# Masked score banks written by ScalarE, queries spread over heads by four transfers a group, and y normalised by GpSimd, in a fused attention and mixture-of-experts layer

## The chip, the cores and the metric

The kernel is one program on one core of a Trainium2 chip. Its time is the device time of one execution in microseconds (us). Three executions of the kernel before took 561.37, 568.28 and 562.6 us, a median of 562.6 us.

## The reference

The input is 4 sequences of 1024 tokens with 256 features, float32. One layer is computed:

```python
x = x + attention(layernorm(x), Wq, Wk, Wv, Wo)   # 16 heads of 16, window of 64 keys, causal
x = x + ffn(layernorm(x), ...)                    # 8 experts, 2 chosen per token, plus a shared expert
# attention: scores = q.k / sqrt(16) + bias; bias is 0 where i-64 < j <= i, else -inf; softmax over j; times v; times Wo
```

Norms have eps 1e-5 and no gain. The router takes the sigmoid of its logits, and an expert's output is scaled by the mean of its tokens' weights. Only the attention part is touched by the change; the experts' part follows it and is the same in both kernels.

## The kernel before

**Tiling.** The attention runs as a sweep over 16 groups `g` of 256 tokens (`step` on every engine, called by `sweep`). A group has 4 blocks `n` of 64 queries; `b = 4g + n` numbers the blocks, 64 in all. A block of 64 queries needs 128 keys, its own 64 and the 64 before. Since the queries of four heads are laid as a block diagonal against the keys (`bd`), a block's scores for 16 heads are one tile of 128 keys x 1024 (head, query) columns. It fills two PSUM banks; there are two such pairs, `S[0]` and `S[1]`, used in turn. In a sequence's first block the first 64 keys are masked out altogether (`mask_first`), in all others the window mask applies (`window_mask`).

**A block on TensorE** (`step`, L726). The scores of block b+1 come first (`scores_of`, L617): two bf16 matmuls write the mask into the banks, for the keys' upper and lower 64 rows (L621), and the products add to it (L626). They wait for `s_P`, the exponentials of block b-1, which had the same banks. Then `shift_of` (L642) subtracts the row maxima from block b. It waits for two transfers that SyncE (SP) issues, of the negated maxima's high and low parts (L331). Then come the products of the probabilities of block b-1 with v (`pv_of`, L656), the first half of a projection for the next group (q at n=0, k at n=1, v at n=2; L567), the transpose of block b+1's maxima (`maxima_T`, L637), the transposes of the products with v (`pvT_of`, L665), the second half of the projection, the output projection (`wo_of`, at n=1 and 2), and the transpose of the block's output (`oT_of`, L671). At n=0 the four transposes of the normalised tokens for the experts stand between `pvT_of` and the second half (`zT_of`, L578); at n=3 those of the tokens for the group after next stand there (`yT_of`, L578), and in the place of a projection the routing logits (L703, L710).

**VectorE** reads the scores for their maxima (L1221, `rmax`), reduces the transposed maxima (L1226, `negm`, and L1229, `neglo`), divides by the softmax sum, forms the low parts of values that are multiplied in two float32r parts (L1194, L1245), and does statistics, residuals and routing. **ScalarE** does the exponentials (L1015), the copies out of PSUM (`pvs` L1022, the high parts L977 and L1027, q, k and v), the copy of the routing logits (L1039, `parts`), at n=3 of groups 2 to 11 a weight cast (L1074, `wF`), the normalisation of y for the group after next (L1033, at n=0), and the spread of q into `bd`: four multiplications of the whole `qs` by a column of ones and zeros per head (L1000; one at n=0, three at n=1). **GpSimd** computes 1/std (L448, L450) and the product that L1033 adds as its bias (L447, L454), the places of routed rows, and issues the indirect transfers that scatter them (L511). SP issues, besides the maxima, at n=1 a load of expert weights (L326) and the store of the transposed tokens (L338).

**Order.** Each engine's instructions stand in the order in which the functions call them; semaphores join the engines. Nothing else reorders them.

## Time and profile before

| | |
|---|---|
| executions (us) | 561.37, 568.28, 562.6; median 562.6 |
| profiled execution (us) | 568.08, span 566.3 |
| granted TensorE clock, mean | 0.976 of full speed |
| busy: PE, VectorE, ScalarE, GpSimd | 93%, 69%, 60%, 40% of the span |
| the sweep over the 16 groups | from about 17 to 334 us of the span |

The span runs from the first to the last instruction of the profiled execution; the rest of its time lies around it. PE is TensorE's matmul, PEld its weight load, DVE VectorE, ACT ScalarE, POOL GpSimd, and SPq the transfers that SyncE issues. An engine's busy time is the sum of its instructions, and says nothing on what it waits for.

### The profile page before, as it was taken

The page shows a single profiled execution, that of the slowest core. Times are in us where ns is not written, and L with a number is a line of the kernel's source. Part 1 is how long each engine was busy: PE and PEld are TensorE (multiplying, and loading weights), DVE is VectorE, ACT ScalarE, POOL GpSimd, SP SyncE. Part 2 cuts the span into 40 slices and gives each one's busy share as a digit, 9 for nine tenths or more (in the row PEclk, how much of TensorE's full clock was granted, in tenths as well). Part 3 has the DMA queues.
Part 4 walks back from the last instruction along what each step waited for, and adds up shares of the span by engine and source line. Part 5 has one row for each costly group of instructions (what it writes and reads, how often), then busy time and mean ns, then how long its engine had stood idle before and what let it go on. Part 6 is the DMA issues. An engine that isn't in the chain of part 4 may idle for free.

```text
span 566.3 us, 16447 instructions
## 1 busy us (share of the span) xinstructions
PE 526.6 (93%) x5561; PEld 422.5 (75%) x5561; DVE 390.3 (69%) x1207; ACT 337.2 (60%) x776; POOL 227.5 (40%) x419
## 2 busy tenths in 40 slices
PE   7899999899999899999989868889999999989997
PEld 4567877676776687677777546878888887769996
DVE  6566688788788788778767646666666665542764
ACT  4667787776777687677676423316676666551111
POOL 5100112244245335424423426723555555443661
PEclk9899999989999999999998977999999999998999
DMA  6260101311321320321121114777555454425994
...
DMA packets 42559, 69.16 MB, mean 122 GB/s; under 512 B 9708, under 2 KB 28655, under 8 KB 42480
## 3 DMA queue, kind: packets, MB, share of 16 engines
...
q14 instruction: 31, 0.25, 0.1%
...
## 4 chain that ended last, share of the span: by engine, by line
PE 80%; ACT 7%; DVE 5%; issue 4%; another core or an unknown queue 2%; DMA 0%; POOL 0%; SPq 0%; ACTq 0%; DVEq 0%; POOLq 0%
PE ps L567 40%; PE ps L626 8%; PE ps L656 6%; PE ps L820 5%; PE ps L911 3%; PE ps L665 3%; PE ps L621 3%; PE ps L578 2%; PE ps L642 2%; ACT probs L1015 2%; PE ps L671 2%; PE ps L710 2%; PE ps L928 1%; ACT vm L988 1%
## 5 line engine op out<-in xcount | busy, mean ns | idle before, releaser
L511 POOL DMA_INDIRECT z_slots<-z,slot x64 | 64.5, 1008 | 120.6 <-PE ps L626 100.3
L567 PE MATMUL ps<-wF,wA 128*128 x639 | 105.6, 304 | 1.7 <-DVE wA L1551 1.0
L552 POOL DMA_INDIRECT y_rows<-vm,dest x71 | 69.6, 980 | 72.5 <-issue 37.8
L567 PEld LDWEIGHTS ps<-wF,wA 128*128 128x128 f32 x639 | 85.2, 189 | 14.3 <-issue 6.2
L1221 DVE TRANSPOSE_TENSOR_REDUCE rmax<-ps 128x32 f32<-128x1024 f32 x64 | 79.6, 1244 | 17.9 <-PE ps L626 16.6
L1015 ACT ACTIVATE probs<-ps 128x1024 f32<-128x1024 f32 x64 | 65.6, 1025 | 34.8 <-PE ps L642 33.9
L626 PE MATMUL ps<-bd,kT 64*128 64x256 f32 x512 | 68.9, 391 | 0.0
L567 PE MATMUL ps<-yT,wA 128*128 128x256 f32 x384 | 61.9, 299 | 1.5 <-DVE yT L1194 1.5
L626 PEld LDWEIGHTS ps<-bd,kT 64*128 64x128 f32 x512 | 51.5, 198 | 5.7
L567 PEld LDWEIGHTS ps<-yT,wA 128*128 128x128 f32 x384 | 50.0, 191 | 4.6 <-issue 1.9
L1119 ACT ACTIVATE vt<-ps 128x256 f32<-128x256 f32 x32 | 12.3, 383 | 56.1 <-PE ps L567 56.1
L1226 DVE TENSOR_REDUCE negm<-ps 32x32 f32<-32x128 f32 x64 | 17.8, 278 | 39.0 <-PE ps L637 29.4
L1551 DVE TENSOR_TENSOR wA<-ps,wA 128x256 fp32r<-128x256 f32 x71 | 30.1, 424 | 20.7 <-issue 11.9
L1000 ACT ACTIVATE bd<-qs,cst 128x512 f32<-128x512 f32 x62 | 43.2, 723 | 0.1
L1160 ACT ACTIVATE vt<-ps 128x128 f32<-128x128 f32 x71 | 19.8, 279 | 38.8 <-PE ps L567 32.4
L1557 DVE TENSOR_TENSOR vt<-vt,ps 128x128 f32<-128x128 f32 x71 | 20.3, 286 | 28.3 <-ACT vt L1160 22.2
L1172 ACT ACTIVATE vm<-ps,tile_w 128x256 f32<-128x256 f32 x71 | 33.8, 476 | 9.6 <-PE ps L567 6.6
L820 PE MATMUL ps<-wD,vt 128*128 128x256 f32 x128 | 32.8, 381 | 1.7 <-issue 1.7
L448 POOL TENSOR_TENSOR rstd<-mv,epsb 128x2 f32<-128x2 f32 x32 | 6.1, 190 | 68.5 <-DVE mv L1206 68.5
L665 PE MATMUL ps<-identf,pvs 128*128 128x128 f32 x126 | 26.6, 293 | 7.5 <-ACT pvs L1022 6.0
L567 PE MATMUL ps<-wA,yT 128*128 128x256 f32 x192 | 30.7, 296 | 0.0
L567 PE MATMUL ps<-wA,wF 128*128 128x256 f32 x192 | 29.8, 307 | 0.6 <-ACT vm L1172 0.6
...
## 6 DMA issues: line engine op xcount, KB each, us to landing
...
```

The lines of the kernel that those rows point to most:

```text
L511: eng.indirect_dma_start(z_slots, bass.IndirectOffsetOnAxis(ap=slot[:, c, j, t:t + 1], axis=0), z[:, c, t, :], None, bounds_check=E * REGI ...
L552: eng.indirect_dma_start(y_rows, bass.IndirectOffsetOnAxis(ap=dest[:, m:m + 1], axis=0), yo[:, m, :], None, bounds_check=K * T - 1, oob_is ...
L567: mm = eng.matmul(out, lhsT(a), rhs(b), start=start and n == 0, stop=stop and n == 2, skip_group_check=skip)
L626: mm = eng.matmul(S[n % 2][:, c, m * QH * WIN:(m + 1) * QH * WIN], kT[rows[c], par, m, n:n + 2, :].rearrange("p a c -> p (a c)"), bd[rows[ ...
L656: mm = eng.matmul(into[32 * i:32 * i + 32, r, :], v[:, par, n // 2, h, :], probs[:, n % 2, h * WIN:(h + 1) * WIN], start=True, stop=True)
L665: mm = eng.transpose(ps[:, pv_bank(b), (KT + c) * P:(KT + c + 1) * P], src[:, c * P:(c + 1) * P], identf[:, :])
L820: mm = eng.matmul(bank(2 + (g + GA) % 2)[:, t, :], hf[:, i % NU, t * P:(t + 1) * P], wD[:, e, :], start=e == 0 and t == 0, stop=e == NS - ...
L1000: spread = eng.activation(bd[:, par, :, :, h, :], qs[:, :].rearrange("p (m n q) -> p m n q", m=KT, n=BPG), ACT.Copy, scale=const("quad")[: ...
L1015: eng.activation(probs[:, n % 2, :], S[n % 2].rearrange("p a c -> p (a c)"), ACT.Exp, scale=HD ** -0.5).then_inc(s_P, 1)
L1172: eng.activation(yo[:, m, :], ps[:, 2 + m % 2, 0:D], ACT.Copy, scale=w).then_inc(s_y1, 1)
L1221: eng.tensor_reduce(rmax[:, n % 2, 0:32], S[n % 2].rearrange("p a (c q) -> p (a c) q", q=32), AX.X, ALU.max, apply_transpose=True).then_in ...
L1551: eng.tensor_tensor(z1[:, m % 2, 1, :], ps[:, 4 + m % 2, 0:D], f(z1[:, m % 2, 0, :]), ALU.subtract).then_inc(s_zl, 1)
```

## The change

The mask becomes a float32 tile `masks` of 128 keys x 64 queries in two versions. ScalarE copies it, repeated over the 16 heads, into the score banks of block b+2 (`seed`), after the exponentials of block b, the copy `pvs` and, at n=3, that of the logits. TensorE's two mask matmuls go; its score products wait for `s_seed` in place of `s_P`. The output dimensions of Wq are permuted so that four heads interleave over the partitions, p % 4 naming the head within a quad. The spread of q is then four transfers a group, each of 32 partitions x 512 values from `qs` to `bd`, which SP issues at n=1 behind that block's maxima; the other partitions of `bd` hold zeros from the start, and `bd` has the head as an outer dimension. The first group's `bd` is still multiplied out. The load of expert weights follows these transfers, and the store of the transposed tokens moves to n=2. GpSimd normalises y at the start of its step, subtracting the mean and multiplying by 1/std, and the two steps for the bias go. On TensorE, `pvT_of` moves between the two halves (by k) of the projection's second half, `zT_of` behind the projection, and `yT_of` ahead of `pvT_of`. The warm-up matmuls write the four score banks once, and ScalarE seeds blocks 0 and 1 ahead of its first weight cast.

```diff
-        bd = sb("bd", [P, 2, KT, BPG, QH, WIN])
+        bd = sb("bd", [P, 2, QH, KT, BPG, WIN])
...
@@ -325,6 +322,14 @@
                     after(eng, s_wFl, 2 * (w - 1))
                     eng.dma_start(wraw_of[:, w % 2, :], wffn[:, weights_at(w), :]).then_inc(s_wf[w % 2], 16)
 
+                def q_by_heads(G, par):
+
+                    if G == 1:
+                        eng.wait_ge(s_bz, 1)
+                    eng.wait_ge(s_qs, G + 1)
+                    for h in range(QH):
+                        eng.dma_start(bd[h:P:QH, par, h, :, :, :].rearrange("p m n q -> p (m n q)"), qs[h:P:QH, :]).then_inc(s_bd, 16)
+
                 def load_mrow(b, pb):
                     for part, (ready, rows) in enumerate(((s_nm, negm), (s_nl, neglo))):
                         eng.wait_ge(ready, b + 1)
@@ -341,6 +346,8 @@
...
+                        if n == 1 and ahead:
+                            q_by_heads(g + 1, 1 - par)
...
-                        if n == 1 and old >= 2:
+                        if n == 2 and old >= 2:
...
-                        eng.tensor_tensor(minus_mean[:, 1, :], minus_mean[:, 0, :], rstd[:, 0, :], ALU.mult).then_inc(s_sh, 1)
+
+                def normalise_y(G):
+                    eng.wait_ge(s_rs[0], G + 1)
+                    eng.wait_ge(s_yTp, G)
+                    for t in range(TPG):
+                        eng.tensor_scalar(y[:, t, :], xs[:, TPG * G + t, :], mv[:, 0, t, 0:1], rstd[:, 0, t:t + 1],
+                                          ALU.subtract, ALU.mult).then_inc(s_yz[0], 1)
 
                 chain(eng.memset(neglo[:, :, :], 0.0))
                 eng.memset(shift[:, :, :], 0.0).then_inc(s_pad, 1)
+                chain(eng.memset(masks[:, :, :], 0.0))
+                chain(eng.memset(masks[0:64, 1, :], MASKED))
+
...
+                eng.memset(bd[:, 1, :, :, :, :].rearrange("p h m n q -> p (h m n q)"), 0.0).then_inc(s_bz, 1)
...
-                    if g and g + 2 < NG:
-                        rstd_of(0, g + 3)
+                    if g + 2 < NG:
+                        if g:
+                            rstd_of(0, g + 3)
+                        normalise_y(g + 2)
...
-                def scores_of(b, par, n, mask):
+                def scores_of(b, par, n):
 
                     rows = [slice(64 * c, 64 * c + 64) for c in range(2)]
-                    for c in range(2):
-                        eng.matmul(S[n % 2][:, c, :].rearrange("p (h q) -> p h q", q=WIN), mask[rows[c], :],
-                                   identb[rows[c], 64 * c:64 * c + 64].unsqueeze(1).to_broadcast([64, HPT, WIN]),
-                                   start=True, stop=False)
+                    eng.wait_ge(s_seed, b + 1)
                     for m in range(KT):
                         for c in range(2):
-                            mm = eng.matmul(S[n % 2][:, c, m * QH * WIN:(m + 1) * QH * WIN],
+                            mm = eng.matmul(S[n % 2][:, c, m * QH * WIN:(m + 1) * QH * WIN].rearrange("p (h q) -> p h q", q=WIN),
                                             kT[rows[c], par, m, n:n + 2, :].rearrange("p a c -> p (a c)"),
-                                            bd[rows[c], par, m, n, :, :].rearrange("p h q -> p (h q)"),
-                                            start=False, stop=m == KT - 1)
+                                            bd[rows[c], par, :, m, n, :],
+                                            start=False, stop=m == KT - 1, skip_group_check=True)
                     mm.then_inc(s_S, 1)
...
-                                eng.wait_ge(s_bd, g + 2)
+                                eng.wait_ge(s_bd, 16 * QH * (g + 1))
                                 eng.wait_ge(s_k, g + 2)
                                 eng.wait_ge(s_halo, g + 1)
-                            if old or n:
-                                eng.wait_ge(s_P, b)
-                            first = n == BPG - 1 and place == GPB - 1
-                            scores_of(b + 1, par2, n2, mask_first if first else window_mask)
+                            scores_of(b + 1, par2, n2)
...
-                        if (old or n) and (ahead or n < 3):
-                            pvT_of(b - 1)
                         if n == 3 and ahead == 2:
                             eng.wait_ge(s_v, g + 2)
                             yT_of(g + 2)
+                        if project:
+                            project(g + 1, (1,), (0,))
+                        if (old or n) and (ahead or n < 3):
+                            pvT_of(b - 1)
+                        if project:
+                            project(g + 1, (1,), (1,))
                         if n == 0 and old >= 2:
                             zT_of(g - 2, (place - 2) % GPB)
-                        if project:
-                            project(g + 1, (1,))
...
-                    for i in range(12):
-                        eng.matmul(ps[:, 2, :], shiftb[:, 0, 0:P, 0], shiftb[:, 1, :, 0], start=True, stop=True)
+                    for i in range(4):
+                        mm = eng.matmul(ps[:, i, :], shiftb[:, 0, 0:P, 0], shiftb[:, 1, :, 0], start=True, stop=True)
+                    mm.then_inc(s_warm, 1)
+                    for i in range(8):
+                        eng.matmul(ps[:, RT, :], shiftb[:, 0, 0:P, 0], shiftb[:, 1, :, 0], start=True, stop=True)
...
+                    after(eng, s_bd, 16 * QH * (G - 1))
                     eng.copy(qs[:, :], ps[:, BANK_A, :]).then_inc(s_qs, 1)
                     eng.wait_ge(s_qs, G + 1)
 
-                def q_by_heads(G, par, heads, last=QH - 1):
+                def first_q_by_heads(heads):
 
                     for h in heads:
-                        spread = eng.activation(bd[:, par, :, :, h, :],
-                                                qs[:, :].rearrange("p (m n q) -> p m n q", m=KT, n=BPG),
+                        spread = eng.activation(bd[:, 0, h, :, :, :].rearrange("p m n q -> p (m n q)"), qs[:, :],
                                                 ACT.Copy, scale=const("quad")[:, h:h + 1])
-                        if h == last:
-                            spread.then_inc(s_bd, 1)
+                    spread.then_inc(s_bd0, 1)
...
+                def seed(b, n, first):
+
+                    after(eng, s_P, b - 1)
+                    eng.copy(S[n % 2].rearrange("p a (h q) -> p (a h) q", q=WIN),
+                             masks[:, int(first), :].unsqueeze(1).to_broadcast([P, HPT * 2, WIN])).then_inc(s_seed, 1)
...
-                def normalise_y(G):
-
-                    eng.wait_ge(s_sh, G + 1)
-                    for t in range(TPG):
-                        eng.activation(y[:, t, :], xs[:, TPG * G + t, :], ACT.Identity, bias=minus_mean[:, 1, t:t + 1],
-                                       scale=rstd[:, 0, t:t + 1]).then_inc(s_yz[0], 1)
 
...
-                        if n == 0 and ahead == 2:
-                            normalise_y(g + 2)
+                        if ahead or n < 2:
+                            seed(b + 2, n, n == 2 and place == GPB - 1)
                         if n == 0 and old >= 2:
                             zT_hi(g - 2, old >= 3)
                         if n == 0 and ahead:
                             q_copy(g + 1)
                         if n == 1 and ahead:
-                            q_by_heads(g + 1, 1 - par, (1, 2))
...
-                        if n == 0 and ahead:
-                            q_by_heads(g + 1, 1 - par, (0,))
                         if n == 1 and ahead:
-                            q_by_heads(g + 1, 1 - par, (3,))
                             eng.wait_ge(s_k, g + 1)
                             eng.copy(kT[:, 1 - par, :, 0, :], kT[:, par, :, BPG, :]).then_inc(s_halo, 1)
...
+                    eng.wait_ge(s_masks, 1)
+                    eng.wait_ge(s_warm, 1)
+                    seed(0, 0, True)
+                    seed(1, 1, False)
                     eng.wait_ge(s_w, 16)
                     weights_hi(0)
...
-    by_heads = (HD * heads[:, None] + np.arange(HD)).reshape(-1)
+    by_heads = (HD * heads[:, None] + np.arange(HD)).reshape(-1, QH, HD).transpose(0, 2, 1).reshape(-1)
...
-        "quad": p[:, None] // HD % QH == np.arange(QH),
+        "quad": p[:, None] % QH == np.arange(QH),
```

TensorE, the block n=0 of a group in the middle (`identf,pvs` are the transposes of the products with v, `identf,z` those for the experts, `identf,rmax` the maxima's). Before:

```order
L621 MATMUL ps<-identb,window_mask 128x512 x2
L626 MATMUL ps<-bd,kT 128x256 x4
L642 MATMUL ps<-shift,onesb 128x512 x2
L656 MATMUL ps<-probs,vt 32x64 x16
L567 MATMUL ps<-yT,wA 128x256 x6
L637 MATMUL ps<-identf,rmax 128x128
L665 MATMUL ps<-identf,pvs 128x128 x2
L578 MATMUL ps<-identf,z 128x128 x4
L567 MATMUL ps<-yT,wA 128x256 x6
L671 MATMUL ps<-identf,o 128x128
```

and now:

```order
L628 MATMUL ps<-bd,kT 128x256 x4
L644 MATMUL ps<-shift,onesb 128x512 x2
L658 MATMUL ps<-probs,vt 32x64 x16
L572 MATMUL ps<-yT,wA 128x256 x6
L639 MATMUL ps<-identf,rmax 128x128
L572 MATMUL ps<-yT,wA 128x256 x3
L667 MATMUL ps<-identf,pvs 128x128 x2
L572 MATMUL ps<-yT,wA 128x256 x3
L583 MATMUL ps<-identf,z 128x128 x4
L673 MATMUL ps<-identf,o 128x128
```

The two mask matmuls are gone, and the four transposes for the experts stand behind the whole projection, where they stood ahead of its second half.

ScalarE, from the copy of the logits at n=3 through n=0 of the next group (`probs<-ps` the exponentials, `yT`, `zT` and `oT` the high parts). Before:

```order
L1039 COPY parts<-ps 16x256
L1074 CAST wF<-wraw_of 128x768
L977 CAST yT<-ps 128x512
L1027 CAST oT<-ps 128x2x64
L1015 ACTIVATE probs<-ps 128x1024
L1022 COPY pvs<-ps 128x256
L1033 ACTIVATE y<-xs,minus_mean,rstd 128x256 x2
L977 CAST zT<-ps 128x512
L994 COPY qs<-ps 128x512
L1027 CAST oT<-ps 128x2x64
L1000 ACTIVATE bd<-qs,cst 128x8x64
```

and now:

```order
L1041 COPY parts<-ps 16x256
L1024 COPY ps<-masks 128x1024
L1075 CAST wF<-wraw_of 128x768
L981 CAST yT<-ps 128x512
L1036 CAST oT<-ps 128x2x64
L1018 ACTIVATE probs<-ps 128x1024
L1031 COPY pvs<-ps 128x256
L1024 COPY ps<-masks 128x1024
L981 CAST zT<-ps 128x512
L999 COPY qs<-ps 128x512
L1036 CAST oT<-ps 128x2x64
```

At n=3 the copy of the mask stands ahead of the weight cast and of `yT`'s high part; at n=0 it takes the place of y's normalisation.

## Rows read from the trace of the kernel before

**Rows 1.** The page's chain that ended last: shares of the span.
```profile
PE 80%; ACT 7%; DVE 5%; issue 4%; another core or an unknown queue 2%; DMA 0%; POOL 0%; SPq 0%; ACTq 0%; DVEq 0%; POOLq 0%
```
**Rows 2.** Busy time by engine in group 7: window, length, PE, PEld, DVE, ACT, POOL, clock.
```profile
155.36:175.58 20.22, 19.44 (x263) 14.85 (x263) 16.43 (x53) 15.16 (x30) 8.24 (x19) 1.00 0.25 76
```
**Rows 3.** Timeline of PE from n=2 of group 7: start, duration, instruction.
```profile
167.96 0.28 PE L637 MATMUL ps<-identf,rmax 128*128 128x128 f32 x1
168.25 0.44 PE L665 MATMUL ps<-identf,pvs 128*128 128x128 f32 x2
170.15 0.39 PE L621 MATMUL ps<-identb,mask_first 64*128 64x512 bf16 x2
...
178.66 0.27 PE L637 MATMUL ps<-identf,rmax 128*128 128x128 f32 x1
178.77 0.38 PE L665 MATMUL ps<-identf,pvs 128*128 128x128 f32 x2
179.15 0.63 PE L578 MATMUL ps<-identf,z 128*128 128x128 f32 x4
179.53 0.96 PE L567 MATMUL ps<-yT,wA 128*128 128x256 f32 x6
180.33 0.27 PE L671 MATMUL ps<-identf,o 128*128 128x128 f32 x1
180.53 0.39 PE L621 MATMUL ps<-identb,window_mask 64*128 64x512 bf16 x2
180.76 1.03 PE L626 MATMUL ps<-bd,kT 64*128 64x256 f32 x8
...
183.34 0.28 PE L637 MATMUL ps<-identf,rmax 128*128 128x128 f32 x1
...
188.16 0.28 PE L637 MATMUL ps<-identf,rmax 128*128 128x128 f32 x1
```
**Rows 4.** Timeline of ACT over the same stretch.
```profile
174.29 0.36 ACT L1039 COPY parts<-ps 16x256 f32<-16x256 f32 x1 [1.11 <-PE ps L703]
174.56 0.83 ACT L1074 CAST wF<-wraw_of 128x768 fp32r<-128x768 f32 x1
175.29 0.57 ACT L977 CAST yT<-ps 128x512 fp32r<-128x512 f32 x1
...
177.25 1.02 ACT L1015 ACTIVATE probs<-ps 128x1024 f32<-128x1024 f32 x1 [1.24 <-PE ps L642]
178.17 0.37 ACT L1022 COPY pvs<-ps 128x256 f32<-128x256 f32 x1
...
179.87 0.59 ACT L977 CAST zT<-ps 128x512 fp32r<-128x512 f32 x1 [0.35 <-PE ps L578]
180.53 0.58 ACT L994 COPY qs<-ps 128x512 f32<-128x512 f32 x1
181.14 0.27 ACT L1027 CAST oT<-ps 128x128 fp32r<-128x128 f32 x1
```
**Rows 5.** Timeline of DVE over the same stretch.
```profile
176.25 0.66 DVE L1194 TENSOR_TENSOR yT<-ps,yT 128x512 fp32r<-128x512 f32 x1
...
177.19 1.24 DVE L1221 TRANSPOSE_TENSOR_REDUCE rmax<-ps 128x32 f32<-128x1024 f32 x1
...
181.44 0.29 DVE L1245 TENSOR_TENSOR oT<-ps,oT 128x128 fp32r<-128x128 f32 x1 [0.26 <-ACT oT L1027]
```
**Rows 6.** Timeline of the maxima's transfers and the matmul that waits for them.
```profile
175.17 0.49 SPq L331 DMA_DIRECT2D shift<-neglo  x1
176.81 0.10 PEld L642 LDWEIGHTS ps<-shift,onesb 64*128 64x128 bf16 x2 [0.38 <-DMA shift<-neglo]
...
184.50 0.50 SPq L331 DMA_DIRECT2D shift<-neglo  x1
```
**Rows 7.** Groups by line: busy, mean ns, idle before, releaser.
```profile
L1000 ACT ACTIVATE bd<-qs,cst 128x512 f32<-128x512 f32 x62 | 43.2, 723 | 0.1
L560 POOL TENSOR_TENSOR bd<-bd 128x512 f32<-128x512 f32 x8 | 11.5, 1442 | 11.8 <-DMA bd<-y_rows 11.7
```

53 lines of the change are left out of this document (19 added, 34 removed).

## The prediction

> **What bounds the kernel now.** I read the chain of waits first: TensorE holds 80% of it, VectorE and ScalarE 12% together [rows 1]. Then a group in the middle of the sweep: of its 20.22 us the matmuls are busy 19.44, ScalarE 15.16, VectorE 16.43, at full clock [rows 2]. So TensorE sets the pace, and the reader could stop there. But the timelines show how near the others are. I cut a group's period at the transposes of the maxima, for each has VectorE's reduction ahead of it: 167.96 (n=2), 178.66 (n=0), 183.34 (n=1), 188.16 (n=2) [rows 3]. The three spans are 10.70, 4.68 and 4.82, together 20.20 us. At n=0 VectorE starts the maxima only at 177.19, because the low part of yT, which began at 176.25, and three small steps stand ahead [rows 5]. It ends at 178.43, and the transpose follows at 178.66: 0.23 us of slack. At n=1 the low part of oT begins at 181.44, kept waiting by ScalarE [rows 5], and the scores end at 180.76 + 1.03 = 181.79 [rows 3]: hardly any slack either. What TensorE saves ahead of these two points counts only as far as the other two engines come earlier as well.
>
> **The mask matmuls.** The pair takes 0.39 us, but the scores start 0.23 us behind it [rows 3], overlapped; 0.23 us a block is what goes. There are 64 blocks: 1 in the prologue, 4 in each of groups 0 to 14, 3 in the last. All of it is 14.7 us.
>
> **TensorE's order.** At n=2 the transposes of the products with v wait: they follow the maxima's by 0.29 us, at n=0 by 0.11 [rows 3]. A half of a half projection in between hides this: 0.18 us off the first span. At n=0 the transposes for the experts start 0.49 us behind the maxima's [rows 3]. Now the second half of the projection, 0.80 us (179.53 to 180.33 [rows 3]), is ahead of them, and the 0.18 may go here too: 1.11 us behind.
>
> **The seed.** No row shows ScalarE writing a mask into PSUM. The nearest is the exponential over the same 1024 columns, which holds ScalarE for 0.92 us (177.25 to 178.17 [rows 4]); the spread of q costs 0.723 for 512 columns [rows 7], 1.45 for 1024, my upper end. I take 0.92: the same engine, count and banks. The Trainium skill, "ScalarE: Activation LUTs", section on what each stage is for, says that ScalarE writes PSUM faster than SBUF. By that rule the seed would be below 0.92, and each 0.1 us below would give 0.1 us in a group with a weight cast, 1 us in all over the ten of them. No run shown so far has such a copy.
>
> **First span, n=2 to n=0.** Everything up to the copy of the logits comes 0.18 + 0.23 = 0.41 us earlier: that copy starts at 173.88 for 174.29, and ScalarE is free 0.27 later [rows 4], at 174.15. Seed to 175.07. Where there is a weight cast, it takes 0.73 (174.56 to 175.29 [rows 4]), to 175.80. The high part of yT takes 0.57, to 176.37, so VectorE's low part starts at 176.40 where it started at 176.25 [rows 5]. The maxima follow 0.94 later as before, 177.34, last 1.24, and the transpose comes at 178.62. From 167.96 that is 10.66 us for 10.70: nothing left of 0.64. Without the cast (groups 12 to 14) the high part is done in time. Then the second transfer of the maxima limits: it is issued at 175.17 and the matmul that wants it starts at 176.81, having waited 0.38 [rows 6]. It is issued 0.41 earlier, so the span is 10.70 - 0.41 = 10.29. The seed itself is done at 174.15 + 1.02 = 175.17. The matmul that waits for the transfer starts at 176.81 - 0.41 = 176.40, and the scores ahead of it need 1.03: they may start as late as 175.37, so the new wait for the seed just fits in.
>
> **Second span, n=0 to n=1.** From the maxima's transpose: transposes for the experts at 1.11; ScalarE's high part 0.72 later (179.15 to 179.87 [rows 3, 4]), 1.83; the q copy 0.5 behind it (0.59, less an overlap of 0.10 such as that of the exponential's 1.02 with 0.92), 2.33; the high part of oT 0.61 behind (180.53 to 181.14 [rows 4]), 2.94; its low part 0.30 behind (181.44 [rows 5]), 3.24, lasting 0.29; the maxima 1.24, and the transpose 0.03 behind: 4.80 us for 4.68. TensorE alone would need 4.68 - 0.23 - 0.18 = 4.27. The ScalarE time freed by y (two ACTIVATEs at n=0) doesn't help, because here ScalarE waits for TensorE [rows 4].
>
> **Third span, n=1 to n=2.** No such chain: 4.82 - 0.23 = 4.59.
>
> **q by transfers.** ScalarE loses four spreads of 0.723 a group [rows 7], 43.2 us busy in all; it was not waited for at n=1, so I count none as gain. SP issues the second maxima transfer of n=1 at 184.50, done 0.50 later [rows 6], and then four issues of 0.5, the last at 186.5. Landing takes 176.81 - 175.17 = 1.64 us for such a small transfer [rows 6], so 188.2. The scores at n=3 want it 2.01 behind the maxima's transpose of n=2, at 183.34 + 4.59 + 2.01 = 189.94: 1.7 us to spare. Behind them in SP's queue the weight load starts 2 us later and is needed over 7 us later; the next maxima's transfers come at about 188.5, when SP is idle again. The tokens' store moves by a block and has the better part of a group left.
>
> **y on GpSimd.** Bounds: nothing that matters, and 2 x 1.44 us, the cost of a two-input operation over twice the columns [rows 7]. y is wanted only at n=3, three blocks later. GpSimd is busy 8.24 of 20.22 us [rows 2]; the scatters move back by 1 to 2 us, and I count nothing. The Trainium skill, "GPSIMD Engine Reference", section "Engine selection", speaks against this move (elementwise work belongs on VectorE, GpSimd is about twice as slow on two inputs). By it the operation is dearer, and the sum is the same while the cover holds.
>
> **The sum.** Groups with a cast, also 2 and 3: 10.66 + 4.80 + 4.59 = 20.05, 0.15 less, x 10 = 1.5 us. Groups 12 to 14: 10.29 + 4.80 + 4.59 = 19.68, 0.52 less, x 3 = 1.6. Groups 0 and 1, without routing and transposes for the experts: 8 x 0.23 = 1.8. Prologue and last group: 4 x 0.23 = 0.9. Together 5.8 us. Against the profiled execution's own 568.1 us that makes 562.3. That one was 5.5 us above the median of the three; from the median of 562.6 it is **556.8 us**.
>
> **The rivals.**
> - *TensorE keeps the pace* (0.25). For it: the chain [rows 1] and the 93% busy; my two chains add up starts to a tenth of a microsecond, and a shorter seed or faster steps on VectorE would break them. All of 14.7 us plus two waits of 0.18 in 14 groups, 5.0: 543; without the latter 548.
> - *The new chains are longer* (0.17). A seed of 1.45 us adds 0.53 in ten groups, 5 us, and a scatter of GpSimd that falls late could add as much as it takes away: 560 to 566, say 562.
> - *The transfers of q come too late* (0.08), slower. If the four transfers don't overlap but land one after the other, as four of 1.64 us from 185.0, the last lands at 191.6, 1.7 us after it is wanted. In 15 groups this is 25 us: 582. It decides from a landing 4.9 us after the first issue on; at 6.1 us it makes the kernel more than 2% slower. For it: nothing shows four such transfers side by side, and they come from and go to every fourth partition. Against: the DMA engines are busy a quarter of the time in such a group [rows 2].
> - *My forecast* (0.50): a gain of 1%, its own range 552 to 561.
>
> **Numbers.** About 2%, 11.3 us, is what a measurement of this kernel can tell from no change. Faster by more (below 551.3): the first rival and a tail of the forecast, 0.28. Slower (above 573.9): the third and a little unforeseen, 0.10. Within: 0.62. For 8 in 10 the range reaches halfway into the first rival and past the second: 546 to 565.
>
> **What would show it.** Right: the period of groups 5 to 11 is 20.0 to 20.1 us, of 12 to 14 about 19.7; the transpose of the maxima at n=0 and n=1 waits for VectorE (rmax), the low part of yT starts right behind ScalarE's high part, and the idle time of yT's high part is small. A seed has a mean near 1.0 us. No weight load of the scores waits for a transfer into bd. Wrong: a period of 19.3 or less with no wait for rmax (first rival); a seed above 1.3 us (second); scores at n=3 waiting for bd (third); a score matmul that takes longer over the new layout of bd than 1.03 us for a block.

## The result and the profile after

The runs fell on several chips, of two kinds. The kernel before takes about 565 us on some (called A here: that of the forecast's runs, whose number is not on record, chip 10 for series 2 and chip 9 for series 3) and about 534 us on others (B: chip 12 for series 1, chip 3 for series 4, chip 1 for series 5). "On A" and "on B" mean a chip of that kind, and only ratios to the kernel before, timed beside each run on the same chip, are compared across the two kinds. A series is one of the sets "Experiments 1" to "5" below.

The change made the kernel slower. On A it takes **589.3 us** (median of 581.29 to 592.65) where the kernel before takes 563.98 beside it: ratio **1.0384, interval 1.0299 to 1.0468**. The ratio leaves out executions in a slower state (two of the four of the changed kernel, and the profiled one of the kernel before), so it is not 589.3 / 563.98. A second measurement gave 1.035 (1.0289 to 1.0411). The forecast of 556.8 us is wrong, and 589.3 lies outside its range. The profiled execution took 587.76 us, with a span of 585.9 us and a mean clock of 0.965.

The page after, for [rows 1]: shares of the chain that ended last, by engine.
```profile
PE 62%; ACT 8%; DMA 8%; DVE 7%; issue 5%; another core or an unknown queue 4%; SPq 3%; POOL 2%; ACTq 0%; POOLq 0%; DVEq 0%
```
TensorE had 80% of the chain and has 62%. DMA had nothing and has 8%. Groups 9, 10 and 11 after, for [rows 2], in the same columns:
```profile
210.15:232.00 21.85, 19.31 (x255) 14.85 (x253) 16.05 (x50) 15.12 (x27) 9.53 (x18) 0.97 0.25 83
232.00:254.52 22.52, 19.78 (x255) 15.47 (x253) 17.20 (x51) 15.24 (x28) 10.01 (x20) 0.93 0.26 80
254.52:276.29 21.77, 18.75 (x255) 14.63 (x255) 16.96 (x51) 15.24 (x29) 10.32 (x20) 1.00 0.25 83
```
A group takes about 22 us, not 20.2, and TensorE is idle 2.5 to 3 us of it. The number behind POOL's is the granted clock: 0.97, 0.93 and 1.00, for 1.00 in [rows 2]. What its matmuls waited for over the whole span:
```profile
PE ps L667 <- ACT pvs L1031: 16.8, 14, 2.2
PE ps L644 <- DMA shift<-neglo: 13.4, 15, 2.8
PE ps L658 <- DVE oT L1247: 7.4, 16, 0.7
```
The numbers are us in total, times, and the longest. The first two lines were 6.0 and 2.7 us before, the third was not there. They are three mechanisms, and each has its place in block n=3 to n=0 of a group. PE, for [rows 3]:
```profile
225.95 0.40 PE L644 MATMUL ps<-shift,onesb 64*128 64x512 bf16 x2 [0.49 <-DMA shift<-neglo]
226.28 0.65 PE L658 MATMUL ps<-probs,vm 128*32 128x64 f32 x32
...
227.46 0.27 PE L639 MATMUL ps<-identf,rmax 128*128 128x128 f32 x1
227.57 0.60 PE L583 MATMUL ps<-identf,y 128*128 128x128 f32 x4
229.59 0.44 PE L667 MATMUL ps<-identf,pvs 128*128 128x128 f32 x2 [1.42 <-ACT pvs L1031]
...
233.02 1.08 PE L658 MATMUL ps<-probs,vt 128*32 128x64 f32 x32 [0.38 <-DVE oT L1247]
```
ACT over the same stretch, for [rows 4]:
```profile
226.40 1.02 ACT L1018 ACTIVATE probs<-ps 128x1024 f32<-128x1024 f32 x1 [0.44 <-PE ps L644]
229.17 0.37 ACT L1031 COPY pvs<-ps 128x256 f32<-128x256 f32 x1 [1.75 <-remote]
229.44 0.36 ACT L1041 COPY parts<-ps 16x256 f32<-16x256 f32 x1
229.70 1.00 ACT L1024 COPY ps<-masks 128x1024 f32<-128x1024 f32 x1
```
DVE, for [rows 5]:
```profile
229.33 0.28 DVE L1228 TENSOR_REDUCE negm<-ps 32x32 f32<-32x128 f32 x1 [2.12 <-remote]
...
231.98 0.69 DVE L1196 TENSOR_TENSOR yT<-ps,yT 128x512 fp32r<-128x512 f32 x1 [0.30 <-ACT yT L981]
232.59 0.28 DVE L1247 TENSOR_TENSOR oT<-ps,oT 128x128 fp32r<-128x128 f32 x1
```
And POOL:
```profile
226.28 0.97 POOL L514 DMA_INDIRECT z_slots<-z,slot  x1 [3.69 <-PE ps L628]
227.55 0.97 POOL L514 DMA_INDIRECT z_slots<-z,slot  x1 [0.30 <-issue]
```
The reader is to see that ScalarE and VectorE stand still until 229.2, although what they wait for from TensorE (the products with v, begun at 226.28, and the transpose at 227.46) is over by 227.8. They go on together, 2.9 us after the first of two scatters (indirect transfers) that GpSimd issues in a row, and 1.6 us after the second; that last distance is 1.56 to 1.63 us in each of groups 4 to 14. "Remote" as a releaser means that the profile shows no instruction of this core that ends the wait. This idle time is called the stall below. The same stall stood in the profile before: it is the 1.11 us ahead of `parts` [rows 4]. There the copy `pvs` had slipped through ahead of it.

The last line of PE shows a fourth effect: the products with v, 0.65 us at 226.28, take 1.08 us at 233.02. The granted clock is 0.50 from 232 to 235 us, behind the stall; the last section shows such a fall by the microsecond.

SPq in the blocks n=1 and n=2 ahead, for [rows 6]:
```profile
218.63 0.49 SPq L336 DMA_DIRECT2D shift<-neglo  x1
219.17 2.42 SPq L331 DMA_DIRECT2D bd<-qs  x4
221.64 0.58 SPq L323 DMA_DIRECT2D wraw_of<-wffn  x1
223.34 0.56 SPq L336 DMA_DIRECT2D shift<-negm  x1
223.95 0.55 SPq L336 DMA_DIRECT2D shift<-neglo  x1
```
The four issues take 0.6 us each. They push the load of expert weights, 384 KB, whose landing takes 3.7 us by the page, to 1.7 us ahead of the next maxima. In the first group the maxima's second transfer is issued at 33.20, behind the four of q and two loads of x, and the matmul waits:
```profile
37.39 0.61 PE L644 MATMUL ps<-shift,onesb 64*128 64x512 bf16 x2 [2.78 <-DMA shift<-neglo]
```

**Where the 19.6 us of span went**, by the first shift matmul of each group: 4.2 by the start of group 1 (42.55 for 38.40), 0.5 in groups 1 to 4, 13.5 in groups 5 to 11 (155.39 us for 141.93), 6.3 in groups 12 to 14, and 4.9 us back behind the last group's start.

The table gives the mean time from one shift matmul to the next in groups 5 to 11, by the block that it leads to, for the kernels of the sections below.

| kernel (kind of chip) | n=0 | n=1 | n=2 | n=3 | group | start of group 1 | mean clock, groups 5 to 11 |
|---|---|---|---|---|---|---|---|
| before (A) | 5.68 | 4.81 | 4.83 | 4.96 | 20.28 | 38.40 | 1.00 |
| changed (A) | 5.99 | 5.69 | 4.93 | 5.59 | 22.20 | 42.55 | 0.97 |
| b_q (A) | 7.29 | 5.23 | 4.80 | 5.58 | 22.90 | 42.12 | 0.92 |
| a_wl (A) | 6.86 | 5.91 | 5.14 | 5.07 | 22.97 | 41.53 | 0.90 |
| a_store1 (A) | 6.16 | 5.35 | 5.04 | 6.91 | 23.46 | 42.31 | 0.88 |
| a_q_st2 (A) | 6.28 | 5.73 | 5.11 | 5.19 | 22.31 | 38.36 | 0.95 |
| a_scat (A) | 4.40 | 5.62 | 4.79 | 5.70 | 20.51 | 42.02 | 1.00 |
| b_scat (B) | 4.59 | 4.69 | 4.77 | 4.77 | 18.81 | 38.59 | 1.00 |
| b_order_scat (B) | 4.48 | 4.89 | 5.13 | 4.76 | 19.26 | 39.99 | 1.00 |
| best1 (B) | 4.45 | 5.29 | 4.95 | 4.72 | 19.41 | 38.21 | 1.00 |
| a_q_scat (B) | 4.52 | 5.29 | 4.93 | 4.64 | 19.38 | 38.98 | 1.00 |
| a_y_scat (B) | 4.34 | 5.28 | 4.99 | 5.63 | 20.25 | 41.76 | 1.00 |

The clock is 1.00 in every one of these groups on B, and on A in `a_scat`. On A it falls in the other versions of the change. What it costs shows in TensorE's busy time, a group: 18.60 us in `a_scat`, 19.34 in the changed kernel, 20.63 in `b_q`, 20.45 in `a_wl`, 20.93 in `a_store1`.

### The profile page after: what moved, and what is told of

It reads as the page before. It is cut to its first block, busy times and chain, and to the rows that moved or that the text cites. A ratio compares the mean times of both kernels' runs of the same rounds, so it can differ in the third digit from the quotient of the medians.

```text
span 585.9 us, 16233 instructions
## 1 busy us (share of the span) xinstructions
PE 523.6 (89%) x5433; PEld 421.8 (72%) x5433; DVE 400.3 (68%) x1207; ACT 344.2 (59%) x752; POOL 255.9 (44%) x411
## 4 chain that ended last, share of the span: by engine, by line
PE 62%; ACT 8%; DMA 8%; DVE 7%; issue 5%; another core or an unknown queue 4%; SPq 3%; POOL 2%; ACTq 0%; POOLq 0%; DVEq 0%
PE ps L572 33%; DMA shift<-neglo 7%; PE ps L628 5%; PE ps L658 5%; PE ps L824 4%; PE ps L915 4%; ACT probs L1018 2%; PE ps L644 2%; PE ps L667 2%; SPq L336 2%; DVE rmax L1223 2%; PE ps L639 2%; ACT ps L1024 1%; PE ps L932 1%
## 5 line engine op out<-in xcount | busy, mean ns | idle before, releaser
L572 PEld LDWEIGHTS ps<-wF,wA 128*128 128x128 f32 x639 | 84.8, 188 | 13.5 <-issue 5.8
L628 PE MATMUL ps<-bd,kT 64*128 64x256 f32 x512 | 77.7, 425 | 0.3 <-ACT ps L1024 0.2
L572 PE MATMUL ps<-yT,wA 128*128 128x256 f32 x384 | 66.4, 312 | 1.8 <-DVE yT L1196 1.8
L1024 ACT COPY ps<-masks 128x1024 f32<-128x1024 f32 x64 | 65.4, 1022 | 0.0
L572 PEld LDWEIGHTS ps<-yT,wA 128*128 128x128 f32 x384 | 53.7, 199 | 5.2 <-DVE wA L1386 2.0
L628 PEld LDWEIGHTS ps<-bd,kT 64*128 64x128 f32 x512 | 46.5, 196 | 13.0 <-issue 4.2
L1228 DVE TENSOR_REDUCE negm<-ps 32x32 f32<-32x128 f32 x64 | 17.8, 278 | 52.6 <-PE ps L639 39.0
L1031 ACT COPY pvs<-ps 128x256 f32<-128x256 f32 x63 | 23.3, 370 | 30.1 <-remote 21.8
L644 PE MATMUL ps<-shift,onesb 64*128 64x512 bf16 x128 | 27.1, 418 | 14.2 <-DMA shift<-neglo 13.4
L1559 DVE TENSOR_TENSOR vt<-vt,ps 128x128 f32<-128x128 f32 x71 | 20.3, 287 | 26.0 <-ACT vt L1162 20.3
L461 POOL TENSOR_SCALAR y<-xs,mv,rstd 128x256 f32<-128x256 f32 x28 | 34.8, 1244 | 1.5
```

Source lines behind the costliest of these rows:

```text
L461: eng.tensor_scalar(y[:, t, :], xs[:, TPG * G + t, :], mv[:, 0, t, 0:1], rstd[:, 0, t:t + 1], ALU.subtract, ALU.mult).then_inc(s_yz[0], 1)
L572: mm = eng.matmul(out, lhsT(a), rhs(b), start=start and n == 0, stop=stop and n == 2, skip_group_check=skip)
L628: mm = eng.matmul(S[n % 2][:, c, m * QH * WIN:(m + 1) * QH * WIN].rearrange("p (h q) -> p h q", q=WIN), kT[rows[c], par, m, n:n + 2, :].re ...
L644: mm = eng.matmul(S[n % 2][:, c, :], onesb[64 * c:64 * c + 64, :], shiftb[64 * c:64 * c + 64, n % 2, :, 1], start=False, stop=True, skip_g ...
L1024: eng.copy(S[n % 2].rearrange("p a (h q) -> p (a h) q", q=WIN), masks[:, int(first), :].unsqueeze(1).to_broadcast([P, HPT * 2, WIN])).then ...
```

## Experiments 1: each part undone (chip 12, kind B)

Four kernels are the changed one with one part as before. The expectations were written against the times on A; the runs fell on B, so the ratios count. `a_y`: y on ScalarE.
```diff
-                        normalise_y(g + 2)        # GpSimd
+                        if n == 0 and ahead == 2:
+                            normalise_y(g + 2)    # ScalarE
```


> The changed kernel with one part undone: y is normalised by ScalarE again (before's L1033), all else as changed. Three theories. (Y) GpSimd's two operations of 1.2 us on y run beside VectorE's normalisation of z at n=0 and stretch it from 0.69 to 1.17 us; the negated maxima, the reciprocals and o stand behind it: undoing gives back about 0.5 us in each of 14 groups, 7 us, about 580 us where the changed kernel has 588. (Q) The q transfers and the weight load behind them make the maxima's transfers land late: then nothing changes here beyond 2 us. (S) The mask copy on ScalarE delays everything behind it: then this is slower than the changed kernel by up to 1 us in a group, about 600 us, as y joins the mask copy at n=0.

Measured: 553.15 us for 533.66, 1.0362 (1.0321 to 1.0402).

`a_q`: q spread by ScalarE, and the tokens' store back at n=1; the new layout of bd stays.
```diff
-                            q_by_heads(g + 1, 1 - par)    # four transfers
-                        if n == 2 and old >= 2:
+                        if n == 1 and old >= 2:
                             store_zt(g - 2)
+                            q_by_heads(g + 1, 1 - par, (1, 2))    # ScalarE
```


> The changed kernel with the spread of q undone: ScalarE multiplies q into bd by head again (bd keeps its new layout, the mask copies stay on ScalarE), SP issues no q transfers, the store of the transposed tokens is back at n=1. (Q) The shift at n=3 no longer waits for the maxima's transfer (0.9 us in 11 groups, 10 us), nor in the first group (4 us): about 575 us, less what ScalarE's 2.9 us of spreads a group cost now that the mask copies are there too; the block n=1 then holds 5.2 us of ScalarE work, about 0.4 us more than TensorE's: up to 6 us back, so 575 to 581. (Y), (S): at 588 or above.

Measured: 539.45 us, 1.0118 (1.0083 to 1.0154).

`a_mask`: TensorE's mask matmuls, no seed.
```diff
-                    eng.wait_ge(s_seed, b + 1)
+                    for c in range(2):
+                        eng.matmul(S[n % 2][:, c, :].rearrange("p (h q) -> p h q", q=WIN), mask[rows[c], :],
```


> The changed kernel with the mask written by TensorE's bf16 matmuls again, no mask copies on ScalarE. (S) The copy at n=3 no longer stands ahead of the high part of yT: the product with the probabilities at n=0 stops waiting 0.74 us for the low part of oT; 14 groups give 10 us, less 0.23 us for each of 64 mask pairs that come back, partly hidden by waits: 580 to 590 us. (Q), (Y): slower than the changed kernel by up to 15 us (0.23 a block), 600 us.

Measured: 553.57 us, 1.0345 (1.0294 to 1.0395).

`a_order`: TensorE's old order.
```diff
-                            project(g + 1, (1,), (0,))
                         if (old or n) and (ahead or n < 3):
                             pvT_of(b - 1)
-                            project(g + 1, (1,), (1,))
...
+                            project(g + 1, (1,))
```


> The changed kernel with TensorE's order of before (transposes of the products with v ahead of those of y, the transposes for the experts ahead of the projection's second half). (O) The transposes for the experts come 0.6 us earlier, so ScalarE's high part, q's copy, oT's parts and the maxima of n=1 do too: 14 groups x 0.3 to 0.6 us, 580 to 584 us. (Q), (Y), (S): within 2 us of the changed kernel's 588, or slower by the 0.18 us waits that come back (5 us).

Measured: 550.09 us, 1.03 (1.0268 to 1.0332).

What follows: the transfers of q are the large part. Without them group 1 starts at 37.5 and not at 42.0 to 42.5, and a group takes 19.4 and not 20.3 us. The other three lie at 1.030 to 1.036, near the 1.035 and 1.038 of the changed kernel on A. The stall of ScalarE and VectorE is in none of these four traces, and their clock is 1.00 in groups 4 to 14. Block n=3 of `a_y`, with the same pair of scatters, first POOL:
```profile
238.38 0.97 POOL L515 DMA_INDIRECT z_slots<-z,slot  x1 [3.66 <-PE ps L627]
239.66 0.97 POOL L515 DMA_INDIRECT z_slots<-z,slot  x1 [0.30 <-issue]
```
and ACT:
```profile
238.73 1.02 ACT L1017 ACTIVATE probs<-ps 128x1024 f32<-128x1024 f32 x1 [0.67 <-PE ps L643]
239.65 0.37 ACT L1030 COPY pvs<-ps 128x256 f32<-128x256 f32 x1
240.00 0.36 ACT L1047 COPY parts<-ps 16x256 f32<-16x256 f32 x1
```
The exponential starts 0.35 us behind the first of the pair, and the copy follows it at once. In groups 5 and 11 of the changed kernel on A it starts 0.57 and 0.74 us behind, and there the copy is held for 1.28 and 1.11 us. The stall belongs to the chips A. As `a_y` is 1.036 here without it, the stall is not what makes the change slow on B.

## Experiments 2: which property of the transfers (chip 10, kind A)

`after_again` is the changed kernel once more.

> The changed kernel once more, on the chip of the next runs, as their yardstick. All theories: 1.03 to 1.045 times the kernel before.

Measured: 584.6 us for 565.8, 1.035 (1.0289 to 1.0411).

`b_q` is the kernel before with the transfers of q, the new layout and the store at n=2.
```diff
+                        if n == 1 and ahead:
+                            q_by_heads(g + 1, 1 - par)    # four transfers
-                        if n == 1 and old >= 2:
+                        if n == 2 and old >= 2:
```


> The kernel before with one part of the change: q goes to its interleaved heads by four transfers a group (new layout of bd, store of the tokens a block later), masks by TensorE, old order, y on ScalarE. Theory Q (the four transfers on SP's queue delay the maxima's transfer behind them, at the start and at n=3): 1.025 to 1.04, with the group that wants them longer, and waits of the shift matmuls for neglo of over 8 us more than in the kernel before. Theory I (the loss needs the whole change together, because the seed and the new order have already used up the slack): 1.00 to 1.015.

Measured: 588.61 us, 1.0419 (1.0325 to 1.0514). On A this part alone costs as much as the whole change; the seed and the new order are not needed for it. But of the 2.6 us that a group grows (table), only 0.6 are at n=3, where the maxima's transfer is waited for, and 1.6 in the span to n=0, where the stall and the lower clock are.

`a_wl` issues the weight load at n=0.
```diff
-                        if n == 1 and 4 <= g < NW + 2:
+                        if n == 0 and 4 <= g < NW + 2:
```


> The changed kernel with one edit: SP issues the load of an expert's weights at n=0, behind that block's maxima, and no longer at n=1 behind the four transfers of q. Theory Q1 (in groups 4 to 11 the weight load is what the maxima's transfer of n=3 queues behind; in groups 12 to 14 without it the wait was 0.2 for 1.15 us): the wait at n=3 falls to 0.2 to 0.4 us, 8 groups by 0.9, 7 us or 1.2% less than the changed kernel, so 1.02 to 1.03. Theory Q2 (the q transfers alone do it): within 0.3% of the changed kernel.

Measured: 593.17 us, 1.0496 (1.0423 to 1.057). The wait at n=3 went as Q1 said: 0.18 to 0.25 us in groups 5 to 11, and the block 5.07 for 5.59 us. The time did not come back. The stalled span to n=0 grew from 5.99 to 6.86, and the clock shows why. Group 7 of `a_wl`, columns as in [rows 2]:
```profile
168.62:192.27 23.65, 21.25 (x255) 16.80 (x253) 16.86 (x51) 15.37 (x27) 9.94 (x20) 0.86 0.23 76
```
It is 0.86 in each of groups 5 to 8, which take 23.6 us. Over groups 5 to 11 TensorE's idle time falls by 0.3 us a group against the changed kernel, and its busy time rises by 1.1. The negated maxima's long waits, 23.6 us in 11 for 13.0 in 6 where the releaser is "remote", say less: with those put down to TensorE it is 55.0 us for 52.0. Right on the wait, wrong on the time. Why the clock fell further here is not shown.

`a_qtiny` transfers 16 numbers a partition instead of 512. It leaves out most of q, so its scores are not those of the layer.
```diff
-                        eng.dma_start(bd[h:P:QH, par, h, :, :, :].rearrange("p m n q -> p (m n q)"), qs[h:P:QH, :]).then_inc(s_bd, 16)
+                        eng.dma_start(bd[h:P:QH, par, h, 0, 0, 0:16], qs[h:P:QH, 0:16]).then_inc(s_bd, 16)
```


> The changed kernel, but each of the four transfers of q carries 16 numbers a partition in place of 512, so most of q never reaches bd (the scores are those of a stale q); their number, place and issue are unchanged. If SP's time to issue them is what costs (0.6 us each), the time stays within 0.3% of the changed kernel. If it is the data they move (the maxima's transfer lands later beside or behind them), the waits for neglo at n=3 and in group 0 go, 1.0 to 1.3 us in groups 4 to 11 and 3 us at the start: 10 to 13 us, 2%, so 1.015 to 1.025.

Measured: 583.72 us, 1.035 (1.0293 to 1.0407), the same as `after_again` beside it. 3.8 MB less are moved, and nothing is gained: the four transfers' data cost nothing. What is left of them is SyncE's time to issue them, still 2.42 us for four, and what that time pushes back.

## Experiments 3: the store, and the pair of scatters (chip 9, kind A)

> The changed kernel with the store of the tokens (zT_scratch<-zT, 512 KB) back at n=1, behind the four transfers of q and the weight load; nothing else. Theory T (the store, moved to n=2, sends its data right when the maxima's transfer of n=3 and the scatters of n=3 want the DMA engines; the copy of the products with v then waits, 16.8 us in 14 groups for 6.0 us before, and the shift matmuls 13.4 for 2.7): both waits fall to near those of the kernel before, 1.00 to 1.015 times the kernel before. Theory Q (the four issues of q on SP are what costs, wherever the store is): 1.03 to 1.04, within 0.5% of the changed kernel.

```diff
-                        if n == 2 and old >= 2:
+                        if n == 1 and old >= 2:
                             store_zt(g - 2)
```
`a_store1` measured: 597.0 us for 565.52, 1.0551 (1.0404 to 1.0698). With the store behind q and the weights the maxima's transfer waits behind both, and the span to n=3 is 6.91 us. In groups 4 to 11 `pvs` waits at most 0.4 us, so the stall of the changed kernel is not what costs here; but the clock is 0.86 to 0.88 in groups 5 to 10.

`b_store2` is the opposite edit, in the kernel before.
```diff
-                        if n == 1 and old >= 2:
+                        if n == 2 and old >= 2:
```


> The kernel before with one edit: the store of the tokens at n=2 in place of n=1. Theory T: most of the loss with nothing else of the change, 1.02 to 1.035, with the wait of the transposes of the products with v (PE for ACT pvs) at 12 us or more where it was 6.0. Theory Q: 0.998 to 1.005.

Measured: 565.24 us, 1.0014 (0.9965 to 1.0062).

`a_q_st2` is `a_q` with the store at n=2.
```diff
-                        if n == 1 and old >= 2:
+                        if n == 2 and old >= 2:
```


> The changed kernel with q spread by ScalarE again (as in the first run that did so, which was 1.012 and had the store back at n=1 as well), but the store left at n=2. Theory T: 1.03 or more, the loss is all there without a single transfer of q. Theory Q: 1.01 to 1.015, as with the store at n=1.

Measured: 582.15 us, 1.0354 (1.0238 to 1.047). Theory T falls with the first two: the store's place costs nothing in the kernel before, and putting it back makes the changed kernel worse. `a_q_st2` came out as T had it, but the run that it was to be compared with, `a_q`, had been on B. Its twin with spread scatters, `a_q_scat` below, has the store at n=2 on B and is 1.0089. What `a_q_st2` adds to that is the stall of A and the lower clock (0.95): with the exponential 0.30 us ahead of the pair, the copy `pvs` is sometimes caught (ACT):
```profile
244.24 1.02 ACT L1014 ACTIVATE probs<-ps 128x1024 f32<-128x1024 f32 x1
247.39 0.37 ACT L1027 COPY pvs<-ps 128x256 f32<-128x256 f32 x1 [2.12 <-remote]
```
and where it is not, the copy of the logits is. So on A the change without a transfer of q (1.0354) costs as much as the whole, as `b_q` did with hardly anything but the transfers. In the kernel before the lead is 0.42 us, and in 8 of the groups 4 to 14 `pvs` slips through; in the other 3 it is late by 0.7.

`a_scat` spreads GpSimd's four scatters.
```diff
-                            if n in (1, 2) and ahead:
-                                eng.wait_ge(s_S, BPG * g + n + 3)
+                            if n in (2, 3) and ahead:
+                                eng.wait_ge(s_S, BPG * g + n + 2)
```


> The changed kernel with GpSimd's four scatters of a group placed otherwise: two at once at the start, one behind the scores in block n=2, and one, no longer two in a row, in block n=3. In n=3, from the group in which the scatters begin, ScalarE's copy of the products with v and VectorE's maxima both stand idle for 1.1 to 2.0 us though TensorE has done what they wait for, and go on together while the pair of scatters is under way. Theory P (the pair holds them up): these idle times go (below 0.3 us), 1.0 to 1.5 us a group in 12 groups, 2 to 3% less than the changed kernel, 1.00 to 1.015 of the one before. Theory D (the stall is the DMA engines' load, not the pair): the stall stays above 0.8 us and the time within 1% of the changed kernel. On a chip that shows no such stall at all this run tells nothing: within 0.5% of the changed kernel.

Measured: 566.36 us, 1.0037 (0.9995 to 1.0079), where the changed kernel had 1.035 and 1.038 on other chips of this kind: 3% less. Block n=3, POOL and then ACT:
```profile
259.35 0.97 POOL L514 DMA_INDIRECT z_slots<-z,slot  x1 [3.73 <-PE ps L628]
```
```profile
260.00 1.02 ACT L1018 ACTIVATE probs<-ps 128x1024 f32<-128x1024 f32 x1 [0.97 <-PE ps L644]
260.92 0.37 ACT L1031 COPY pvs<-ps 128x256 f32<-128x256 f32 x1
```
Here the one scatter holds nothing up, though the exponential starts 0.65 us behind it. That is not so in every group: in six of groups 4 to 14 `pvs` waits 0.26 to 0.60 us and starts 1.44 to 1.50 us behind the scatter. So one scatter can hold ScalarE up too, but the pair held it for 1.1 to 2.1 us, and without the pair the long stall and the fall of the clock are both gone. In the changed kernel on A the pair in this place is their cause. The span to n=0 is 4.40 us for 5.99, and also for 5.68 in the kernel before.

## Experiments 4 and 5: the parts without the pair (chips 3 and 1, kind B both times)

> The kernel before with the scatters spread as in the run that did so to the changed kernel; nothing else. Theory P (there the pair falls between ScalarE's copy of the products with v and its next work, for which nobody waits): the idle time of 1.1 us ahead of ScalarE's copy of the logits goes, the time stays, 0.99 to 1.00. Theory C (the pair costs every kernel the same, 2 to 3%): 0.97 to 0.98.

The edit is that of `a_scat`, in the kernel before. Measured: 533.29 us for 534.21, 0.9987 (0.9971 to 1.0003). As the trace has no stall, this does not decide between P and C. The same edit on another chip:

> The kernel before with the scatters spread, once more. If this chip shows the stall in the kernel before: its groups 4 to 14 fall from 20.2 us to 18.8 us, 11 groups by 1.4, 15 us and the last groups beside, so 0.965 to 0.975, and it beats both kernels (theory P2: the pair set the pace of the kernel before there, beside TensorE). Rival (the stall lies beside TensorE's work, and 20.2 us is what this chip's TensorE needs): 0.995 to 1.00. On a chip without the stall: 0.997 to 1.001 whichever holds.

Measured: 533.1 us for 533.63, 0.999 (0.997 to 1.0011). That chip was of kind B too.

`a_q_scat` is `a_q_st2` with spread scatters.
```diff
+                            if n in (2, 3) and ahead:
+                                eng.wait_ge(s_S, BPG * g + n + 2)
```


> The changed kernel with q spread by ScalarE, the store left at n=2 (that was 1.035), and the scatters spread. Against the changed kernel with spread scatters (1.0037) this is the price of the four transfers of q by themselves. Theory Q' (they cost 3.6 us at the start, where the first group's maxima wait behind them, and 0.2 to 0.5 us a group after): 0.985 to 0.995. Theory N (with the pair gone they cost only the start): 0.995 to 1.00.

Measured: 538.85 us, 1.0089 (1.0063 to 1.0116), slower than either theory had it. Both took the 1.0037 of `a_scat`, from A, for a yardstick on B, where the kernel before pays no stall.

`a_y_scat` is `a_y` with spread scatters (the same edit).

> The changed kernel with y on ScalarE again and the scatters spread. Theory Y (GpSimd's y costs: VectorE's normalisation of z takes 1.2 for 0.7 us beside it): 0.5 us a group in 14 groups at the most, 0.99 to 1.00. Theory H (hidden): 1.00 to 1.007, as with y on GpSimd; if ScalarE is short of time at n=0, up to 1.01.

Measured: 551.35 us, 1.032 (1.0298 to 1.0343), above all that was expected, for the same reason. With the transfers and without the stall, this trace tells what the transfers need in order to cost. PE at n=3 of groups 11 and 12:
```profile
258.64 0.40 PE L643 MATMUL ps<-shift,onesb 64*128 64x512 bf16 x2 [0.98 <-DMA shift<-neglo]
277.86 0.40 PE L643 MATMUL ps<-shift,onesb 64*128 64x512 bf16 x2
```
Group 11 has a weight load behind the four transfers, group 12 has none. From the issue of the maxima's second transfer to this matmul it is 2.85 us in group 11 and 1.70 in group 12. In all of groups 5 to 11 it is 2.4 to 2.9 us and the span to n=3 is 5.4 to 5.8; in groups 1, 2, 3, 12 and 13, which have the four transfers and nothing large behind them, it is 1.7 and 4.65 to 4.67, as without the transfers (4.6 to 4.7 in `a_q_scat`). Groups 12 and 13 as a whole take 19.42 and 19.02 us, 19.37 and 19.04 in `best1` below, which has no transfers of q. So in the steady groups the four issues cost nothing by themselves. They cost by the large load that follows them.

`best1` keeps the seed and the new order only: the edits of `a_y` and `a_q` together, the old layout of bd, and spread scatters.
```diff
-        bd = sb("bd", [P, 2, QH, KT, BPG, WIN])
+        bd = sb("bd", [P, 2, KT, BPG, QH, WIN])
```


> The kernel before with two parts of the change, ScalarE's mask in place of the mask matmuls and the new order of TensorE, and with the scatters spread; q by ScalarE, the old layout of bd, y on ScalarE. Theory G (my forecast's chains hold: ScalarE and VectorE give back most of what TensorE saves): 0.98 to 0.99. Theory E (without the pair the chains have room, TensorE keeps the pace): 14.7 us and the waits, 0.965 to 0.975. Theory 0 (the seed brings nothing): 0.995 to 1.00.

Measured: 539.49 us, 1.011 (1.008 to 1.0141). Slower than the kernel before; all three theories had it at 1 or below.

`b_order_scat` is `best1` with TensorE's masks, so that only the order is new, and with it the permuted heads.
```diff
-                    eng.wait_ge(s_seed, b + 1)
+                    for c in range(2):
+                        eng.matmul(S[n % 2][:, c, :].rearrange("p (h q) -> p h q", q=WIN), mask[rows[c], :],
```


> The kernel before with TensorE's new order and the scatters spread; the masks by TensorE, q by ScalarE, y on ScalarE, old layout of bd. Theory SE (the seed is what costs 0.6 us a group, as the order only moves work that is there anyway): within 0.3% of the kernel before with spread scatters, 18.8 us a group. Theory O (the order, by which the transposes for the experts come later, costs): 19.2 us or more a group, 0.8 to 1.1% above the kernel before with spread scatters.

Measured: 539.87 us for 533.63, 1.011 (1.0087 to 1.0134). Theory O. The order alone costs what `best1` costs, and the seed adds nothing that the total shows (0.15 us a group). The profile shows where, in blocks n=0 and n=1. PE of `b_order_scat`:
```profile
231.97 0.39 PE L644 MATMUL ps<-shift,onesb 64*128 64x512 bf16 x2
232.56 0.66 PE L658 MATMUL ps<-probs,vt 128*32 128x64 f32 x32 [0.20 <-DVE oT L1255]
...
236.83 0.40 PE L644 MATMUL ps<-shift,onesb 64*128 64x512 bf16 x2
237.54 0.65 PE L658 MATMUL ps<-probs,vm 128*32 128x64 f32 x32 [0.31 <-DVE oT L1255]
```
and PE of `b_scat`:
```profile
231.19 0.39 PE L642 MATMUL ps<-shift,onesb 64*128 64x512 bf16 x2
231.51 0.65 PE L656 MATMUL ps<-probs,vm 128*32 128x64 f32 x32
```
Behind the shift matmul the products with v started after 0.32 us. Now they start after 0.59 and 0.71, for they want the low part of oT (`eng.wait_ge(s_oTl, b)` in `pv_of`), and it comes late. At the second place DVE shows why:
```profile
236.32 0.69 DVE L1204 TENSOR_TENSOR zT<-ps,zT 128x512 fp32r<-128x512 f32 x1 [0.47 <-ACT zT L981]
237.11 0.29 DVE L1255 TENSOR_TENSOR oT<-ps,oT 128x128 fp32r<-128x128 f32 x1
```
The transposes for the experts stand behind the projection now, so zT's low part comes late, and oT's, which stands behind it on VectorE in either order, with it.

The score matmuls, by line: `b_scat` (masks by TensorE, old layout), `a_mask` (masks by TensorE, new layout) and `best1` (seed, old layout):
```profile
L626 PE MATMUL ps<-bd,kT 64*128 64x256 f32 x512 | 66.5, 380 | 0.0
```
```profile
L640 PE MATMUL ps<-bd,kT 64*128 64x256 f32 x512 | 66.6, 380 | 0.0
```
```profile
L616 PE MATMUL ps<-bd,kT 64*128 64x256 f32 x512 | 73.4, 406 | 0.0
```
The columns are busy us and mean ns of one. The layout costs nothing. Without a mask pair ahead of them, the eight take 1.13 us and not 1.03.

## Why the prediction was wrong, by its steps

- **Mask matmuls, 0.23 us a block.** Mis-sized. TensorE is busy 18.45 us in a group of `best1` and 18.69 in one of `b_order_scat` (groups 5 to 11): 0.06 us a block. That is net of the 0.10 by which the eight score matmuls grow. In time it is worth nothing: 1.011 with the seed and without.
- **The seed, 0.92 us.** Right. It lasts 1.02 us on the mean, and the next instruction starts 0.95 us behind it (229.70, the cast at 230.65). The score matmuls waited for it 0.2 us in the whole span. The rival with a dearer seed did not come true. That ScalarE writes PSUM faster than SBUF (the Trainium skill, "ScalarE: Activation LUTs", section "Step-by-step: what each stage is for") does not show here: the exponential of the same size, into SBUF, lasts 1.02 us too.
- **TensorE's order, 0.18 us off the first span and perhaps off the second.** Wrong in sign. It costs 0.45 us a group (19.26 for 18.81). The chain that I followed ended at the transpose of the maxima. I left out the products with v of the next block, which want oT's low part. That holds for this order without the transfers; in a kernel that has them, going back to the old order gains nothing in these groups (`a_order` 20.36 us, `a_y` 20.29 and `a_mask` 20.37).
- **y on GpSimd, nothing.** Right: `a_q_scat`, with it, is 1.0089, `best1`, without it, 1.011. In the changed kernel the operation takes 1.24 us, and VectorE's normalisation of z 0.50 for 0.39 beside it. In time the cover held. Two of these operations follow each other by 1.23 us, where VectorE does the same for z in 0.39, three times faster. The Trainium skill, "GPSIMD Engine Reference", section "Engine selection", calls one-input operations on GpSimd roughly line-rate; this trace does not agree.
- **q by transfers, "1.7 us to spare", and behind them "the weight load starts 2 us later and is needed over 7 us later".** This is the step that failed most. The scores hardly ever waited for bd. What I took for costless was the load's *flight*: pushed back 2.4 us, its 384 KB are under way when the maxima's transfer of n=2 is issued. From issue to matmul that transfer takes 2.0 us in the group shown and 1.9 to 2.6 in groups 5 to 11, for 1.64 [rows 6]. Where no load follows, in groups 1 to 3 and 12 to 14, it takes 1.7. The Trainium skill, "DMA: Bandwidth & Descriptors", section "Queues, rings and completion order", says that a DMA engine takes a queue's descriptors in the order of the ring; the trace fits that, as a small transfer lands late behind a large one, though it does not show the order on one DMA engine. On B the transfers cost 0.84 us a group (`a_y_scat` 20.25 for `best1` 19.41), and at the start 3.6 us, which I had not looked at: SyncE's queue of the first group holds the loads of x as well.
- **First span.** I took the start of the logits' copy, 174.29 [rows 4], as set by TensorE, and moved it with TensorE. It stood behind 1.11 us of idle time "<-PE ps L703", although that matmul group is over long before. That idle time was the stall, and the row said so. On A it goes from 1.1 us, beside which TensorE has work, to 1.1 to 2.1 us ahead of `pvs`, for which TensorE waits. The sum also kept the clock at that of the kernel before, 1.00 in the middle groups; behind these stalls it fell, to 0.97 on the mean of groups 5 to 11, and TensorE's busy time in a group rose to 19.34 us where `a_scat` has 18.60.
- **The rivals.** The slower one named q's transfers as too late for the scores. The culprit was right, the victim wrong: the maxima's transfer behind them. It had 0.08 and the range did not reach it.

Added one after the other on B, in groups 5 to 11, the order costs 0.45, the seed 0.15, y and layout 0, the transfers with the load behind them 0.84, together 1.44 us; the start adds 3.2. These are steps from kernel to kernel, and another sequence would share them out otherwise: taken out of the whole, the transfers give back 0.9 (`a_q` 19.38 for `a_y` 20.29), the order and the seed nothing. Spans by the two profiles: `a_y_scat` 550.3, `b_scat` 532.5, 17.8 us more, of which groups 5 to 11 hold 10.0. On A the group grows by 1.92 to 2.25. The part beyond 1.44 is, I take it, the stall's and the clock's: both are worse after the change than before, and the spread scatters take 1.7 to 2.0 us off the changed kernel's group (20.51 for 22.20 and 22.53), more than the 1.1 to 1.3 estimated below for the kernel before. No run shows that split, and on A the parts do not add up: `b_q` and `a_q_st2`, which share almost no part of the change, each cost as much as all of it.

One reading of mine fell on the way. After `a_scat` I held the stall for the cause of the loss. But it was in the kernel before too, and B shows nearly the same ratio without it. `a_scat` takes away what, by the rows, both kernels pay.

**Open.** Whether the kernel before with spread scatters is faster on A. Its span to n=0 (5.68 there, 4.40 in `a_scat` there, 4.59 in `b_scat` on B) suggests 1.1 to 1.3 us a group, some 12 us; both runs of it fell on B. The two kinds of chip differ beyond the sweep as well: from the start of the last group to the end the kernel before takes 246 us on A, `b_scat` 231 on B. No version shown beats the kernel before by 2%. Why the pair stops two other engines on A, and why a pair in block n=1 of `a_scat` does not, is not known. Nor is it shown why the clock falls behind some stalls and not behind others. The changed kernel itself was not run on B.
